# A four-layer graph network on one core: the attention layer's projection in two passes, and its first 24 gathers issued within the projection stage

## What is computed

```python
x_l = (x @ W_l).reshape(n, H, C)          # x is the layer-normalised input
x_r = (x @ W_r).reshape(n, H, C)
e = (ea @ W_e).reshape(-1, H, C)
m = leaky_relu(x_l[src] + x_r[dst] + e, 0.2)
alpha = einsum('ehc,hc->eh', m, att)      # then a softmax over the edges of a node
out = segment_sum(x_l[src] * a[:, :, None], dst)
```

## Time and profile before

| what | value |
|---|---|
| median of three runs | 2253.06 us (2252.19 to 2255.97) |
| the profiled execution | 2240.74 us |
| its span, first to last instruction | 2239.0 us |
| granted TensorE clock, mean share | 0.872 |
| busy share: TensorE, VectorE, ScalarE, GpSimd | 81%, 60%, 47%, 38% |
| projection, about | 821.8 to 849.4 us |
| attention, about | 849.4 to 2144 us |

### The profile page before, as it was taken

How to read it: one execution, slowest core, us unless ns; L and a number is a source line. 1 busy time by engine, 2 the same in 40 slices (tenths; PEclk the granted TensorE clock), 3 DMA queues, 4 the chain that set the end, 5 groups by cost and what they waited for, 6 DMA issues and landing times. The chain is left out here.

```text
span 2239.0 us, 35303 instructions
## 1 busy us (share of the span) xinstructions
PE 1810.4 (81%) x10709; PEld 1263.7 (56%) x10709; DVE 1335.6 (60%) x3119; ACT 1058.5 (47%) x2333; POOL 848.7 (38%) x886
## 2 busy tenths in 40 slices
PE   5677799979999983768887888887888888888766
PEld 2567765557888752435555555555555555555554
DVE  6999967674333353945555655455655555555585
ACT  0689877645423351224444444444444444444465
POOL 1000000010000015766666666666666666666500
PEclk9555589999999997878898899999899999899987
DMA  3100000014300012323332323233232332333311
GB/s 95 37 1 1 2 8 0 0 29 128 115 1 5 2 33 75 91 70 82 82 83 78 83 80 83 79 81 85 76 83 77 83 82 77 87 80 83 80 34 29
DMA packets 132486, 133.22 MB, mean 60 GB/s; under 512 B 29049, under 2 KB 102354, under 8 KB 132306
## 3 DMA queue, kind: packets, MB, share of 16 engines
q1 hardware_dynamic: 104530, 73.76, 11.4%
q0 software_dynamic: 27776, 57.20, 10.5%
HBM read 126.05 MB, written 4.82 MB: 58 GB/s over the span
## 5 line engine op out<-in xcount | busy, mean ns | idle before, releaser
L2198 POOL DMA_INDIRECT rows<-x_l,src x856 | 823.8, 962 | 460.6 <-issue 226.3
L2323 ACT ACTIVATE bent<-psum 128x512 f32<-128x512 f32 x214 | 127.5, 596 | 609.3 <-remote 343.7
L2284 PE MATMUL psum<-both,node_hot 128*128 128x144 f32 x1712 | 302.0, 317 | 68.2 <-issue 53.6
L2284 PEld LDWEIGHTS psum<-both,node_hot 128*128 128x128 f32 x1712 | 260.8, 209 | 144.1 <-issue 123.9
L2471 DVE TENSOR_TENSOR acc<-acc,psum 128x144 f32 x428 | 127.6, 298 | 285.4 <-remote 244.4
L2216 PEld LDWEIGHTS psum<-hot,x_r_parts 128*128 x1284 | 132.5, 103 | 250.9 <-issue 228.6
L2338 ACT ACTIVATE apart<-iota,rel 128x128 bf16<-128x128 f32 x856 | 270.8, 389 | 2.3 <-PE psum L2284 2.2
L2216 PE MATMUL psum<-hot,x_r_parts 128*128 128x256 bf16 x1284 | 200.9, 293 | 87.6 <-DVE hot L2377 48.2
L2236 PE MATMUL psum<-bent,att_heads 128*128 128x512 f32 x428 | 243.6, 660 | 5.0 <-DVE bent L2381 3.3
L2219 PE MATMUL psum<-edges,w_e 128*128 128x512 f32 x428 | 237.0, 636 | 4.3 <-issue 4.2
L2381 DVE TENSOR_TENSOR bent<-psum,bent 128x512 f32<-128x512 f32 x214 | 146.8, 686 | 112.7 <-issue 78.8
(11 more groups left out here) (344 smaller groups left out, 2397.0 us busy)
## 6 DMA issues: line engine op xcount, KB each, us to landing
rel_row<-e_rel_rows SPq DMA_DIRECT2D x107, 256.0 KB
edges<-edge_t SPq DMA_DIRECT2D x428, 32.0 KB
rows<-x_l,src POOLq DMA_INDIRECT x856
edge_part<-edge_t SPq DMA_DIRECT2D x40, 320.0 KB, 3.1
new<-e_new_before SPq DMA_DIRECT2D x26, 64.0 KB
new<-e_new_behind SPq DMA_DIRECT2D x26, 64.0 KB
ht<-x SPq DMA_DIRECT2D x6, 256.0 KB, 2.8
x_l<-rows SPq DMA_DIRECT2D x4, 320.0 KB
```

What stands on the lines that cost most here:

```text
L2198: e.indirect_dma_start(rows[:, g % ring, j * ROW:(j + 1) * ROW], None, k.xl, bass.IndirectOffsetOnAxis(ap=src[:, at:at + 1], axis=0)).then ...
L2284: final = e.matmul(to, near_hot[:, at, j, :], both[:, at, j, :], start=j % 2 == 0, stop=j % 2 == 1)
```

## The change

The matmul of a block now makes `x_l` alone (128 columns). Even blocks are copied by VectorE, odd ones by ScalarE. When all 25 blocks are through, a second pass makes `x_r`, four blocks to a bank, seven bankfuls in all, and ScalarE copies a whole bank at once. VectorE does the first split after that. GpSimd, in place of the split, waits for the tables and for all stores of `x_l` and issues the 24 gathers of groups 0 to 5 within the projection's block; the attention's own list begins with group 6. The semaphores of the gathers now last over both stages.

```diff
+GOT = 6
 class EdgeTables:
+        self.got = [k.lasting("rows_got") for _ in range(GOT)]
+        self.rows = rows
+    def gather(self, e, g):
+        for j in range(4):
+            at = 4 * g + j
+            e.indirect_dma_start(
+                self.rows[:, g % RING, j * ROW:(j + 1) * ROW], None, self.k.xl,
+                bass.IndirectOffsetOnAxis(ap=self.src[:, at:at + 1], axis=0)).then_inc(*self.got[g % GOT].up(16))
 def project(...):
+        four = 4
+        fours = [(lo, min(lo + four, s.nb)) for lo in range(0, s.nb, four)]
             @block.sync
-                    e.wait_ge(kept.sem, kept.at(hi))
+                    await_kept(e, hi)
             @block.gpsimd
-                e.wait_ge(kept_r.sem, kept_r.at(5))
-                row_parts.split(e, 0, split)
+                e.wait_ge(tables.loaded.sem, tables.loaded.at(tables.here))
+                e.wait_ge(tables.stored.sem, tables.stored.at(tables.stored.n))
+                for g in range(GOT):
+                    tables.gather(e, g)
             @block.scalar
-                    e.wait_ge(kept.sem, kept.at(b + 1))
-                    e.activation(xr[:, b, :], k.bank[4 + b % 4][:, ROW:2 * ROW], ACT.Copy).then_inc(*kept_r.up())
+                    e.wait_ge(projected.sem, projected.at(b + 1))
+                    e.activation(xl[:, b, :], k.bank[4 + b % 4][:, 0:ROW], ACT.Copy).then_inc(*kept_odd.up())
-                    if b >= 3:
+                    if b >= 3 and b % 2 == 0:
                         keep(b - 3)
+                for g, (lo, hi) in enumerate(fours):
+                    e.wait_ge(projected_r.sem, projected_r.at(g + 1))
+                    e.activation(xr[:, lo:hi, :].rearrange("p b f -> p (b f)"), k.bank[g % 4][:, 0:(hi - lo) * ROW],
+                                 ACT.Copy).then_inc(*kept_r.up())
             @block.tensor
-                        e.matmul(k.bank[4 + c % 4][:, 0:2 * ROW], ut[:, c * P:(c + 1) * P], both,
+                        e.matmul(k.bank[4 + c % 4][:, 0:ROW], ut[:, c * P:(c + 1) * P], raw[:, 0, :],
                                               start=True, stop=True).then_inc(*projected.up())
+                for g, (lo, hi) in enumerate(fours):
+                    if g >= 4:
+                        e.wait_ge(kept_r.sem, kept_r.at(g - 3))
+                    for b in range(lo, hi):
+                        last = e.matmul(k.bank[g % 4][:, (b - lo) * ROW:(b - lo + 1) * ROW], ut[:, b * P:(b + 1) * P],
+                                        raw[:, 1, :], start=True, stop=True)
+                    last.then_inc(*projected_r.up())
             @block.vector
-                    if b >= 2:
+                    if b >= 2 and b % 2 == 0:
                         e.wait_ge(projected.sem, projected.at(b - 1))
-                        e.tensor_copy(xl[:, b - 2, :], k.bank[4 + (b - 2) % 4][:, 0:ROW]).then_inc(*kept.up())
+                        e.tensor_copy(xl[:, b - 2, :], k.bank[4 + (b - 2) % 4][:, 0:ROW]).then_inc(*kept_even.up())
+                e.wait_ge(kept_r.sem, kept_r.at(2))
+                row_parts.split(e, 0, split)
 def attention(...):
             @block.gpsimd
-                e.wait_ge(loaded.sem, loaded.at(here))
-                e.wait_ge(tables.stored.sem, tables.stored.at(tables.stored.n))
-                for g in range(groups):
+                for g in range(GOT, groups):
-                    if g >= slots:
-                        e.wait_ge(joined.sem, joined.at(g - slots + 1))
+                    e.wait_ge(joined.sem, joined.at(g - GOT + 1))
```

More of the change, by code:

```diff
@@ L1843, in project, with await_kept @@
         ahead.flags()
-        projected, kept, kept_r = k.flag("projected"), k.flag("x_l_kept"), k.flag("x_r_kept")
+        projected, projected_r, kept_r = k.flag("projected"), k.flag("x_r_projected"), k.flag("x_r_kept")
+        kept_even, kept_odd = k.flag("x_l_kept_even"), k.flag("x_l_kept_odd")
         split = k.flag("x_r_split")
-        both = raw[:, 0:2, :].rearrange("p j f -> p (j f)")
+        four = 4
+        fours = [(lo, min(lo + four, s.nb)) for lo in range(0, s.nb, four)]
+        def await_kept(e, n):
+            e.wait_ge(kept_even.sem, kept_even.at((n + 1) // 2))
+            if n > 1:
+                e.wait_ge(kept_odd.sem, kept_odd.at(n // 2))
         with k.nc.Block() as block:
@@ L1909, in _ @@
                         if c >= 4:
-                            e.wait_ge(kept_r.sem, kept_r.at(c - 3))
+                            await_kept(e, c - 3)
                         if c == 3:
                             e.wait_ge(mean_kept.sem, mean_kept.at(1))
-                        e.matmul(k.bank[4 + c % 4][:, 0:2 * ROW], ut[:, c * P:(c + 1) * P], both,
+                        e.matmul(k.bank[4 + c % 4][:, 0:ROW], ut[:, c * P:(c + 1) * P], raw[:, 0, :],
                                               start=True, stop=True).then_inc(*projected.up())
+                for g, (lo, hi) in enumerate(fours):
[5 more added lines that the diff above has]
+                    last.then_inc(*projected_r.up())
             @block.vector
@@ L2088, in attention @@
         ready, own_here, owns = k.flag("attention_ready"), k.flag("own_rows_here"), k.flag("own_logits")
-        got = [k.flag("rows_got", True) for _ in range(slots)]
+        got = tables.got
         edge_here, rel_here = [k.flag("edges_here") for _ in range(edge_slots)], [k.flag("rel_here") for _ in range(slots // 2)]
@@ L2191, in _ @@
                         e.wait_ge(owns.sem, owns.at(cuts))
-                    if g >= slots:
-                        e.wait_ge(joined.sem, joined.at(g - slots + 1))
+                    e.wait_ge(joined.sem, joined.at(g - GOT + 1))
                     if g >= ring:
                         e.wait_ge(weighted.sem, weighted.at(g - ring + 1))
-                    for j in range(4):
-                        at = 4 * g + j
-                        e.indirect_dma_start(
-                            rows[:, g % ring, j * ROW:(j + 1) * ROW], None, k.xl,
-                            bass.IndirectOffsetOnAxis(ap=src[:, at:at + 1], axis=0)).then_inc(*got[r].up(16))
+                    tables.gather(e, g)
             @block.tensor
@@ L2222, in join @@
                     z = z_banks[g % 2]
-                    e.wait_ge(got[g % slots].sem, got[g % slots].at(4 * lap(g)))
+                    e.wait_ge(got[g % GOT].sem, got[g % GOT].at(4 * 16 * (g // GOT + 1)))
                     for j in range(4):
```

1 line of the change is left out of this document (removed).

## The result

The changed kernel takes 2261.28 us (median of 8 runs, 2258.33 to 2263.07), the kernel before 2254.06 us beside it (8 runs), the ratio is 1.0027 with an interval of 1.0018 to 1.0035: 7.2 us slower.

What follows compares the result with a forecast made beforehand. TensorE and the handoffs around it were taken to set the steady pace, GpSimd at its limit of six groups ahead. Group 8's 2.9 us delay plus 0.2 us gave +3 us, 2256 us; range 2240 to 2272, the forecast's own 2251 to 2261.

Steps and rivals of the forecast that it cites:

- The loop of x_l: Projection loop: two blocks take 1.27 us instead of 1.84; with the tail 4.7 us gained, bounds 0 and 5.2.
- The stores: From the last x_l copy to the first gather: 4.5 us for the last stores stay, first gather at 848.0.
- The 24 gathers: Gathers of groups 0 to 5 at the projection's end: they take 30.3 us and end, with the stage, at 878.3.
- the port: VectorE's split slowing gathers that it meets in the projection: taken as 0.2 us.
- What they cover: Under the gathers: the x_r pass, its copies and the split end before 863 and cost nothing.
- The start of attention: From the stage's end to TensorE's first matmul of group 0: 8.0 us, so at 886.5, 30.0 us later than before.
- What is late next: After the seam: VectorE 1.3 us late at bend 4, GpSimd 2.9 us late at group 8; the later sets the end.
- (a): VectorE in attention's steps 0 to 3, 4.23 us each: bend 4 at 908.1, 1.3 us later than before.
- (b): GpSimd stands before group 6 from 878.3 to 890.5, waiting for the first join; group 8 starts 2.9 us later.
- Late word again: Rival, chance 0.27: just after the seam a late word of a join adds 10 us; +13, 2266 us.
- Gathers set the end: Rival, chance 0.18: attention hangs on GpSimd's start, its pause is made up, the 4.7 us come through; -5, 2248 us.
- The second stand goes too: Rival, chance 0.15: ScalarE's 20.14 us wait at group 17 vanishes; -17, 2236 us.

Runs made afterwards that it cites:

- e4: The changed kernel run again with no edit; 2057.30 us against 2045.16 us for the kernel before, ratio 1.0057.
- e3: The changed kernel with all five splits made by VectorE in the projection, under the gathers; 2057.61 us, ratio 1.0052 to the kernel before.
- e5: The changed kernel with 12 gathers (groups 0 to 2) issued in the projection instead of 24; 2046.65 us, ratio 1.0002 to the kernel before.
- e6: The changed kernel with twelve gather semaphores instead of six, a lead of twelve groups; 2047.20 us, ratio 1.0010 to the kernel before.
- e9: Two-pass projection, all gathers in attention, with two of each group's four gathers left out from group 24 on; 1897.64 us, ratio 0.8468 to the kernel before.
- e10: The changed kernel with a lead of twelve groups, on a chip of the slower kind; 2506.52 us, ratio 1.1097 to the kernel before.
- e0: The kernel before, run again unchanged as control; 2047.45 us against 2045.67 us.

## Why the prediction was right, and where its steps were off

The forecast held: the time is inside the range and 7.2 us above before, where I had +3; the forecast's own upper end was +8. The mechanism, a pause of GpSimd ahead of its 25th gather that outweighs the earlier start, was there where I had it, and on the faster kind of chip it is shown to be the cost; the sum was short by 4 us, and one of its terms came out right by luck. Point by point:

- *The loop of x_l.* The sum is right, by luck. 4.7 us predicted; from the projection's first normalisation (821.86 before, 822.89 after) to the end of the last copy of x_l pass 26.3 us before and 21.7 after, 4.6 less. But 2.4 of them were won by the tenth block, where I had nothing, and from there to the last block's normalisation only 1.9 (13.4 us before, 11.5 after), where I had about 4. The 1.27 us for two blocks came true, with 1.31, only at the loop's end. Before that two blocks took 1.65 at half the clock, which the prediction had nowhere. In e4's trace the clock was full from the fifth microsecond to the loop's end; there the last normalisation starts 17.7 us after the first one, not 19.5, and the first gather 24.4 us after it, not 26.3.
- *The stores.* 4.5 predicted, 4.56 measured. The first gather came at 849.17, not 848.0, of which 1.0 us is the later start of the projection in this execution.
- *The 24 gathers.* 30.3 us predicted, 29.7 measured; no gather was long. Most of the split was over before them, and the first gather (849.17, 0.96 us) met the end of a cast and a tensor_tensor that began after it (849.31). My 0.2 us for the port was 0. The 1.6 us that the prediction works out for two casts would not have come either: e3 shows that it is the tensor_tensors that cost, 0.47 us each at the most. The long gather of the earlier trace rows, at 879.09, lay beside such a tensor_tensor (878.85 to 879.67) and no cast.
- *What they cover.* Right: TensorE's pass 5.75 us, copies to 850.45, all hidden.
- *The start of attention.* 8.0 us predicted from the end of the stage to TensorE; 888.43 - 878.83 = 9.6 measured. This term was too small by 1.6 us: from the last gather's end to attention's first instruction on VectorE pass 3.7 us, from the last copy in before 1.8.
- *What is late next.* (a) Bend 4 came at 909.85 (predicted 908.1), the step of 4.23 us held; where gathers set the pace it did not matter (e3, e4). (b) was the right one: GpSimd stood 13.7 us, where I had 12.2 (878.3 to 890.5), and e5 and e6 show that this pause is the cost where gathers set the pace. Group 8 was 4.8 us late counted from the projection's start, not 2.9. Its working: from the first gather to the 25th 43.35 us (849.17 to 892.52) instead of 42.5, the pause 1.5 us longer and the 24 gathers 0.6 shorter, and then 11.33 us for two groups instead of 10.4, with three long gathers near the splits instead of the one I had allowed for. **Mis-sized by 1.9 us** in all: 1.8 from these, 0.1 from the first gather. What follows to 7.2 us grew after group 8, where I had nothing change, and what made it grow is not shown: by group 24 its slope was 6.65 us late by the same count (204.75 us before, 211.40 after).
- *Late word again.* Such waits of 6.9 and 14.15 us did fall into groups 5 and 6. By the rival's own condition it had come true, yet the time is 7.2, not 13. Before had waits of 9.8 and 27.9 us there, so after has fewer and shorter ones. The rival priced the waits of after without crediting those of before. e4 is slower still, by 12 us, with none of them; whether they are part of the 7.2 us on the other kind of chip is not shown.
- *Gathers set the end.* The premise is right on one kind of chip: there every pause of GpSimd comes through to the end. The sign I drew from it was wrong: the 4.7 us won at the start are outweighed by the 13.7 us pause. The difference, 9.0 us, lies at the low end of what e4 measured (8.6 to 14.7 us by its interval). The Trainium skill, DMA: Bandwidth & Descriptors, Rules for kernel authors, asks to issue a DMA early and to wait for it late; the runs show what it leaves to the kernel: e5, which issues half as many groups early, costs nothing, and e4, which issues all of its lead early, costs 12 us.
- *The second stand goes too.* It moved and shrank: at group 17 the slope is 5.0 us late, but at group 15 the join ended at 967.86 and its slope started at 980.43, 12.6 us later, where the earlier trace rows has 20.14 us of idle time. No 17 us were won by it.

Where the statement "the steady pace is set by TensorE and the handoffs around it" stood, e9 and e10 put another: on this kind of chip the handoffs are slow because of the gathers issued beside them.

## What to carry to other kernels

Before you move a queue's work ahead of a stage boundary, count its lead: what is issued early uses it up, and then the boundary's whole restart (here 3.7 us to VectorE's first instruction, 5.9 to TensorE's, 4.1 to the release by the first join) falls on that queue. Move only so much that the queue still has something it may issue when the boundary opens; where gathers set the pace, three groups of six cost nothing and six of six cost 12 us. And don't take a longer lead as free slack: try it on more than one chip, for the burst that it allows can hold up the very engines that free the buffers.

## What the runs showed of the hardware

The same kernel runs in 2045 us on some chips (3, 13 here) and in 2241 to 2256 us on others (6 and 8), each within 0.4% of itself; four chips are few to call them kinds. On the first kind no slope came more than 2.4 us behind its join, on the second they came up to 28 us late (before, group 2), often some 2 to 2.6 us after GpSimd's stream had paused (2.0 in after, 2.55 and 2.57 in e10), but not always: the slope of group 1 of before started in the midst of an unbroken stream. By e9 and e10 the indirect DMAs issued back to back keep TensorE's word to ScalarE back on that kind. ScalarE does not look too late: the trace also records when a semaphore is raised, and for `joined` it has 874.59 and 897.73 in before, each 0.02 us ahead of the slopes of groups 1 and 2, though the joins end by their rows at 864.78 and 869.89. In e0 each record stands 0.01 to 0.02 us behind the row's end, and there are 214 of them for 214 joins, in before only 197. What in the chip does it, whether TensorE's work itself ends late (its ends are modelled) or only its word, and why only some chips show it, stays open. Nor was a lead shorter than six tried, which by e10 may be faster on the slower kind; on the other GpSimd never stopped at a lead of six, so nothing could be won there.

Two more things the traces show. A gather that GpSimd issues while VectorE is in a tensor_tensor with both inputs in SBUF ends only 0.82 us behind that tensor_tensor if more than 0.12 us of it are left (e3; 1.41 us instead of 0.94 where 0.59 us were left), and a cast of f32 to bf16 beside it holds nothing. And TensorE's granted clock was part of the size of a loop's gain: with 0.50 for 10.2 us the same projection loop took 1.9 us longer (after) than with the full clock (e4).
